# 20 of the edge list's columns taken out of the node table in SBUF by TensorE, and two exponentials inside expert group 3

## The chip, the cores and the metric

The kernel runs on one core of a Trainium2 chip. The metric is the device time of one execution in microseconds; lower is better. The median of 3 runs before the change is 858.64 us.

## The reference, cut to what matters

The model has two layers over 4096 tokens of 64 features (64 images of 64 tokens): wavelet tokens, attention, a mixture of dense experts, a recurrent attention, and at the end a graph step with gated experts. Only the last part is touched.

```python
h = (x_flat @ W_gat).reshape(M, HEADS, NUM_EXPERTS)
e = leaky_relu(a_src[src] + a_dst[dst])            # one row for each edge
ee = exp(e - segment_max(e, dst)[dst])
agg = segment_sum(h[src] * alpha, dst)             # alpha = ee / segment_sum(ee, dst)
scores = layernorm(agg + b_gat).reshape(M, HEADS, NUM_EXPERTS).mean(1)
w = softmax(top_k(scores, 2))
out = sum over 4 experts of w_e * (gelu(x @ W1[e] + b1[e]) @ W2[e] + b2[e])
```

There are 262144 edges drawn over 16384 nodes; the nodes past the 4096 tokens are all alike and are handled apart.

## The kernel before

An earlier stage sorts the edges by destination. Each of the 128 partitions owns 32 nodes (`NC`) and has a list of up to 192 places (`PART`), one edge in each, in the order of the destination. A column of the list is one place on all 128 partitions. In this execution 39 groups of 4 columns (`ASK`) hold edges.

Each node has a row of 24 values (`ROW`): 16 of `h`, 4 source scores and 4 destination scores. The rows are in SBUF, `node_rows_own` in the trace (`G.tab`), node 32p + c at partition p, chunk c; and in HBM, `node_table`. Source rows come from HBM: for each column GpSimd issues one indirect DMA (L2051), which brings 128 rows of 96 bytes into `gathered` (`Gt`). After the last chunk has been written out, 32 more (L2062) bring the rows at the segments' ends.

VectorE does, in this order: a merge over the nodes (`merge`, to L2282), four register reads (`value_load`), then `nodes_of_list` (L2286 to L2312: one-hots of list place against node, counts, and the destination's score for each place, four products over 6144 elements and four sums), then `rows_of_chunk` for three chunks of 64 columns (L2325 to L2350), and for each half of the nodes the merge, the gates and the mixing of the experts' outputs. A chunk waits for its columns (`gat[j]`); then come scores, an exponential on ScalarE (`weights`, L2145), and the running sums (L2342 to L2350), which need the exponential.

Beside that TensorE and ScalarE compute the four experts, without regard to the gates, in four groups of 1024 tokens: `layer1` (L2079), gelu (`hidden`, L2128), `layer2` (L2089), the bias by feature (L2134), the turn back to tokens (L2096) and the copy (`keep_tokens`, L2140). TensorE's order is fixed: layer 1 runs one group and two experts ahead of layer 2. ScalarE's order is fixed as well: the exponential of chunk 0 stands in group 3 behind its first gelus, those of chunks 1 and 2 behind all experts. An engine executes its stream in order; a step that waits holds back all behind it.

## Time and profile before

| | us |
|---|---|
| median of 3 runs (858.08 to 859.08) | 858.64 |
| the profiled execution | 853.77 |
| its span | 851.9 |
| VectorE busy | 601.8 (71%) |
| TensorE matmuls busy | 428.7 (50%) |
| ScalarE busy | 269.5 (32%) |
| GpSimd busy | 189.9 (22%) |

The busy share is a mean over stages that have nothing in common. The last 350 us are the stage of the graph and the experts, and there no engine is busy throughout. Such a stage is read by order of time: for a row, when it starts, how long it takes, and in brackets how long the engine stood idle before it and what ended that. Ends of matmuls are modelled by the profiler, while the start of the step that waits for them is recorded. The name behind an arrow can be "remote" or that of an unrelated transfer where the profile could not match the semaphore.

### The profile page before, as it was taken

To read this page: it belongs to the slowest core of one execution; us is meant where nothing else is said; L and a number is where in the kernel's file an instruction comes from. 1 tells how busy PE (TensorE), PEld (TensorE's weight loads), DVE (VectorE), ACT (ScalarE), POOL (GpSimd) and SP (SyncE) were. 2 spreads that over 40 slices of the span, in tenths; PEclk is the share of its full clock that TensorE was granted. 3 is DMA by queue.
4 is the path that set the end of the run, shared out by engine and by line. 5 is a ranking of instruction groups with operands and counts; after the bars stand their busy time and mean duration, and the time that the engine had idled before them with its cause. 6 is when DMAs were issued, how large, how long until landed. Compare 5 with 4: busy or idle time off the path is not lost.

```text
span 851.9 us, 10421 instructions
## 1 busy us (share of the span) xinstructions
PE 428.7 (50%) x3409; PEld 304.7 (36%) x3409; DVE 601.8 (71%) x2087; ACT 269.5 (32%) x589; POOL 189.9 (22%) x202
## 2 busy tenths in 40 slices
PE   5995575766383669969769827610340110600000
PEld 5874575746372135646657413200110000200000
DVE  3999999977698999877797686999400000670487
ACT  2599678256111222224001324400100001600155
POOL 0100000000000000002000027777777770007600
PEclk9998787896595879988798956955555555655555
DMA  9100000010000000001000000111111130011102
GB/s 200 35 2 1 2 2 2 1 29 2 4 2 0 1 1 2 1 1 32 1 1 1 1 22 9 11 10 10 10 10 10 10 10 1 38 74 9 10 0 49
DMA packets 26681, 13.11 MB, mean 15 GB/s; under 512 B 21161, under 2 KB 25833, under 8 KB 26353
## 3 DMA queue, kind: packets, MB, share of 16 engines
q1 hardware_dynamic: 17696, 9.04, 4.2%
q0 software_dynamic: 6016, 2.32, 3.8%
q10 hardware_dynamic: 2904, 0.98, 0.8%
q8 instruction: 29, 0.48, 0.2%
q14 instruction: 36, 0.29, 0.1%
HBM read 8.43 MB, written 3.90 MB: 14 GB/s over the span
## 4 chain that ended last, share of the span: by engine, by line
another core or an unknown queue 17%; DVE 14%; PE 12%; issue 6%; ACT 3%; POOL 2%; DMA 1%; DVEq 0%; ACTq 0%; POOLq 0%
PE bank L2079 2%; DVE state_x L1780 2%; PE bank L1542 2%; POOL node_rows L2062 2%; PE bank L2089 2%; PE bank L1562 1%; DVE state_x L1777 1%; DVE segment_rows L2347 1%; ACT masked_scores L2128 1%; PE bank L1625 1%; PE bank L1614 1%; PE bank L1602 1%; ACT v_sums_and_norms L2134 1%; DVE v_sums_and_norms L2433 1%
## 5 line engine op out<-in xcount | busy, mean ns | idle before, releaser
L2051 POOL DMA_INDIRECT gathered<-node_table,list_src_i x156 | 151.5, 971 | 153.5 <-issue 153.5
L437 ACT ACTIVATE dst_one_hot<-dst_lo,sign_edges 128x256 bf16<-128x256 bf16 x224 | 90.8, 519 | 16.8 <-PE bank L496 16.8
L2342 DVE TENSOR_TENSOR segment_rows<-gathered,edge_weight_and_decay 128x1024 f32<-128x1024 f32 x3 | 3.7, 1225 | 126.8 <-ACT edge_weight_and_decay L2145 126.8
L496 PE MATMUL bank<-dst_one_hot 128*128 128x128 bf16 x1024 | 72.2, 244 | 38.2 <-DVE dst_one_hot L566 38.2
L496 PEld LDWEIGHTS bank<-dst_one_hot 128*128 128x128 bf16 x1024 | 70.9, 112 | 39.6 <-DVE dst_one_hot L566 39.2
L566 DVE TENSOR_SCALAR dst_one_hot<-dst_hi 128x256 bf16<-128x256 bf16 x512 | 76.3, 388 | 0.3 <-ACT edge_keys_then_tokens L421 0.3
L2096 PE MATMUL bank<-ident,v_sums_and_norms 128*128 128x128 f32 x64 | 13.3, 342 | 98.9 <-ACT v_sums_and_norms L2134 61.9
L2079 PE MATMUL bank<-h_features,e_w 64*128 64x512 f32 x64 | 35.7, 955 | 49.3 <-issue 32.5
L2096 PEld LDWEIGHTS bank<-ident,v_sums_and_norms 128*128 128x128 f32 x64 | 8.5, 169 | 114.4 <-ACT v_sums_and_norms L2134 72.4
L2062 POOL DMA_INDIRECT node_rows<-segment_table,segment_end_i x32 | 30.5, 953 | 73.7 <-DMA segment_table<-segment_rows 64.3
L1080 ACT ACTIVATE z_then_h<-bank,e_B,e_A 128x512 f32<-128x512 f32 x32 | 23.0, 774 | 65.1 <-PE bank L901 65.1
L566 DVE TENSOR_SCALAR dst_one_hot<-dst_lo 128x256 bf16<-128x256 bf16 x288 | 43.0, 390 | 0.0
L2134 ACT ACTIVATE v_sums_and_norms<-bank,e_b_by_feature 128x512 f32<-128x512 f32 x16 | 11.0, 687 | 98.7 <-remote 76.7
L2312 DVE TENSOR_REDUCE edge_dst<-v_sums_and_norms 128x192 f32<-128x6144 f32 x4 | 41.9, 10486 | 0.1
L2079 PEld LDWEIGHTS bank<-h_features,e_w 64*128 64x128 f32 x64 | 13.5, 273 | 67.7 <-issue 40.9
L1206 DVE CUSTOM_DVE_ANT_0 rank_prod_then_keyed<-bank,bin_one_hot 128x128 f32<-128x128 f32 x160 | 34.5, 286 | 0.3 <-DVE slot_key L1198 0.3
L879 POOL PARTITION_ALL_REDUCE bin_max_all<-bin_max x1 | 0.3, 350 | 141.2 <-DVE bin_max L1220 141.2
L926 PE MATMUL bank<-h_and_v_then_places,rank_prod_then_keyed 128*128 128x192 bf16 x320 | 30.4, 257 | 2.2 <-DVE rank_prod_then_keyed L1266 1.9
L926 PEld LDWEIGHTS bank<-h_and_v_then_places,rank_prod_then_keyed 128*128 128x128 bf16 x320 | 28.2, 103 | 8.6 <-DVE rank_prod_then_keyed L1266 6.5
L461 POOL PARTITION_ALL_REDUCE left_max<-left_keys x1 | 0.4, 352 | 137.3 <-DVE left_keys L587 137.3
L2089 PE MATMUL bank<-masked_scores,e_w 128*64 128x512 f32 x64 | 23.6, 855 | 14.1 <-issue 14.1
L2140 ACT COPY state_x<-bank 128x512 f32<-128x512 f32 x16 | 9.3, 584 | 60.2 <-remote 48.7
(452 smaller groups left out, 1071.2 us busy)
## 6 DMA issues: line engine op xcount, KB each, us to landing
gathered<-node_table,list_src_i POOLq DMA_INDIRECT x156
segment_table<-segment_rows SPq DMA_DIRECT2D x3, 768.0 KB, 3.2
dst_one_hot<-in_L_ffn_edge_index SPq DMA_DIRECT2D x2, 1024.0 KB, 7.1
out_dram<-edge_keys_then_tokens SPq DMA_DIRECT2D x4, 256.0 KB, 2.9
images_then_col_weights<-in_x SPq DMA_DIRECT2D x2, 441.0 KB
images_then_col_weights<-in_x ACTq DMA_DIRECT2D x2, 441.0 KB
e_w<-in_L_ffn_W SPq DMA_DIRECT2D x6, 128.0 KB, 4.1
node_rows<-segment_table,segment_end_i POOLq DMA_INDIRECT x32
```

Source lines behind the costliest of these rows:

```text
L437: ins = act.activation(hot[q % 2][:, :, 64 + HOTS + k, :], x, ACT.Sign, bias=edge[:, k:k + 1])
L496: ins = pe.matmul(G.bank[0][:, 0:P], hot[u][:, b, 0:64, i:i + PAIR], hot[u][:, b, 64:P, i:i + PAIR], start=False, stop=True, skip_group_ch ...
L566: ins = dve.tensor_scalar(hot[q % 2][:, :, at + v, :], x, float(v), None, ALU.is_equal)
L926: ins = pe.matmul(sent[:, k * SENT_RANKS:(k + 1) * SENT_RANKS], keyed[:, q % SEND_BUFS, k, i, :], place[:, q % SEND_BUFS, i, :], start=Fal ...
L1080: act.activation(H1[:, n % 2, u, :], G.bank[2 * (n % 2) + u][:, :], ACT.Relu, bias=w.par["B1"][:, q:q + 1], scale=w.par["A1"][:, q:q + 1]) ...
L1206: o.mark(dve.tensor_tensor_reduce(out=prod[:, t, :], in0=count, in1=hot[:, c, :], scale=1.0, scalar=0.0, op0=ALU.mult, op1=ALU.add, accum_ ...
L2051: pool.indirect_dma_start(Gt[:, j, :], None, A["table"], bass.IndirectOffsetOnAxis(ap=G.src_i[:, j:j + 1], axis=0)).then_inc(gat[g // per_ ...
L2062: pool.indirect_dma_start(N[:, c, :], None, A["ends"], bass.IndirectOffsetOnAxis(ap=end_i[:, c:c + 1], axis=0)).then_inc(ends_in[c // H2], 16)
L2079: pe.matmul(G.bank[2 * (n % 2) + u][:, :], W1[r, e, :], G.hT[r, g * TILE:(g + 1) * TILE], start=True, stop=True).then_inc(l1_mm, 1)
L2089: ins = pe.matmul(G.bank[5 + i % 3][rows_of(e), :], W2[:, 2 * pair + e, :], HH[:, u, 2 * pair + e, :], start=True, stop=True, skip_group_c ...
L2096: ins = pe.transpose(G.bank[5 + i % 3][:, h * P:(h + 1) * P], G.by_feature[:, i % 3, h * P:(h + 1) * P], G.ident[:, :])
L2312: f.then(dve.tensor_reduce(AD[:, h, :], by_node.rearrange("p c n -> p n c"), AX_X, ALU.add))
```

## The change

Of the 156 columns that hold edges, 20 (places 4 to 23: `PICK`, groups 1 to 5, `PC` = 4, `PK` = 20) are no longer fetched by GpSimd. They are read from `node_rows_own` in SBUF by matrix products. The number of a source row is split into partition (`low`) and chunk (`high`). TensorE turns `low`, spreads each column over all partitions (20 matmuls), and VectorE compares with the partition's number, which gives a one-hot [node partition x list partition] for each column. For each column two matmuls multiply it with the table's 768 values, into two banks; VectorE multiplies by the one-hot of the chunk and sums over the 32 chunks, which gives the column in `gathered`. All of it stands in VectorE's stream ahead of `nodes_of_list`, and in TensorE's behind the layer-1 matmuls of group 0 and ahead of those of group 1. GpSimd's loop over earlier passes (none in this execution) is split from the last pass, which leaves the 20 columns out, and chunk 0 waits for 20 columns fewer (`asked[NCH]`).

In ScalarE's stream the exponential of chunk 1 moves into expert group 3, behind the gelus of expert 2. The waits for the experts' copies are split by half of the nodes, and `G.gate_tmp` lies in another quarter of the same tile.

```diff
+PICK = range(1, 6)
+PC, PK = PICK.start * ASK, len(PICK) * ASK
...
-    G.gate_tmp = lnv[:, :, :].rearrange("p c d -> p (c d)")[:, 0:3 * NC * 16].rearrange("p (i c f) -> p i c f", i=3, f=16)
+    G.gate_tmp = quarters[:, 0, 0:3 * NC * 16].rearrange("p (i c f) -> p i c f", i=3, f=16)
...
+                if g in by_pe:
+                    continue
...
+        last = passes_but_last(pool)
+        with pool.If(last > 0):
+            with pool.Fori(0, last) as k:
+                list_rows(k, ())
+                node_rows(k)
+        list_rows(last, PICK)
+        node_rows(last)
...
+        def pick_rows():
+
+            pe.wait_ge(gelu_s, 2 * EXP1)
+            pe.wait_ge(low_s, 1)
+            pe.transpose(G.bank[0][0:PK, 0:P], low[:, :], G.ident[:, :]).then_inc(low_mm, 1)
+            pe.wait_ge(lowT_s, 1)
+            for b in range(len(PICK)):
+                for i in range(4):
+                    ins = pe.matmul(G.bank[SPREAD[b]][:, i * P:(i + 1) * P],
+                                    G.ident[0:PK, 4 * b + i:4 * b + i + 1].to_broadcast([PK, P]), low_T, start=True,
+                                    stop=True, skip_group_check=True)
+                ins.then_inc(spread_mm, 1)
+            for j in range(PK):
+                pe.wait_ge(hot_s, 1 if j == 0 else len(PICK))
+                if j >= 3:
+                    pe.wait_ge(pick_s, j - 2)
+                for i, b in enumerate(pick_banks(j)):
+                    ins = pe.matmul(G.bank[b][:, 0:NC // 2 * ROW], hot_rows[:, j, :],
+                                    flat_tab[:, i * (NC // 2 * ROW):(i + 1) * (NC // 2 * ROW)], start=True, stop=True)
+                ins.then_inc(pick_mm, 1)
+            pe.wait_ge(pick_s, PK)
...
         for n in range(NG * EXP1):
+            if n == EXP1:
+                pick_rows()
             layer1(n)
...
-            act.wait_ge(x_s, 4 * NG)
+            act.wait_ge(x_s, 2 * NG * (g + 1))
...
                 hidden(g, e)
+                if g == NG - 1 and e == 2:
+                    weights(last, 1)
...
-        for j in range(1, NCH):
-            weights(last, j)
+        weights(last, NCH - 1)
...
+    def pick_rows_of_list(dve, f):
+
+        c = slice(PC, PC + PK)
+        f.mark(dve.tensor_scalar(low_i[:, :], G.src_i[:, c], 5, None, ALU.arith_shift_right))
+        f.then(dve.tensor_scalar(high_i[:, :], G.src_i[:, c], NC - 1, NC, ALU.bitwise_and, ALU.bitwise_or))
+        f.then(dve.tensor_copy(low[:, :], low_i[:, :]))
+        f.mark(dve.tensor_copy(high[:, :], high_i[:, :]))
+        f.then(dve.tensor_scalar(low[:, :], low[:, :], float(PART), None, ALU.mult))
+        dve.sem_inc(low_s, 1)
...
+        for j in range(PK):
+            dve.wait_ge(pick_mm, j + 1)
+            for i, b in enumerate(G.pick_banks(j)):
+                h = slice(i * (NC // 2), (i + 1) * (NC // 2))
+                f.mark(dve.tensor_tensor(picked[:, j % 2, :, h],
+                                         G.bank[b][:, 0:NC // 2 * ROW].rearrange("p (c f) -> p f c", f=ROW),
+                                         hot_high[:, j, h].unsqueeze(1).to_broadcast([P, ROW, NC // 2]), ALU.mult))
+            f.wait()
+            dve.sem_inc(pick_s, 1)
+            f.mark(dve.tensor_reduce(Gt[:, PC + j, :], picked[:, j % 2, :, :], AX_X, ALU.add))
+        f.wait()
...
+        pick_rows_of_list(dve, f)
         nodes_of_list(dve, f)
-        rows_of_chunk(dve, f, last, 0, asked[0])
+        rows_of_chunk(dve, f, last, 0, asked[NCH])
...
-        dve.wait_ge(x_s, 4 * NG)
         merge_half(dve, f, last, 0)
```

TensorE, from the turn of the tokens to the first layer-2 steps of the experts; the number behind x counts matmuls in a row. Before:

```order
L2109 MATMUL bank<-ident,e_b 128x1 x2
L2079 MATMUL bank<-h_features,e_w 128x512 x12
L2089 MATMUL bank<-masked_scores,e_w 64x512 x4
L2096 MATMUL bank<-ident,v_sums_and_norms 128x128 x4
L2089 MATMUL bank<-masked_scores,e_w 64x512 x2
L2096 MATMUL bank<-ident,v_sums_and_norms 128x128 x4
L2089 MATMUL bank<-masked_scores,e_w 64x512 x2
L2096 MATMUL bank<-ident,v_sums_and_norms 128x128 x8
```

After:

```order
L2164 MATMUL bank<-ident,e_b 128x1 x2
L2108 MATMUL bank<-h_features,e_w 128x512 x8
L2143 MATMUL bank<-ident,picked_row_low 20x128
L2147 MATMUL bank<-v_sums_and_norms,ident 128x128 x20
L2156 MATMUL bank<-node_rows_own,v_sums_and_norms 128x384 x40
L2108 MATMUL bank<-h_features,e_w 128x512 x4
L2118 MATMUL bank<-masked_scores,e_w 64x512 x4
L2125 MATMUL bank<-ident,v_sums_and_norms 128x128 x4
L2118 MATMUL bank<-masked_scores,e_w 64x512 x2
L2125 MATMUL bank<-ident,v_sums_and_norms 128x128 x4
```

One transpose, 20 spreading matmuls and 40 picking ones stand between the eighth and the ninth layer-1 matmul.

VectorE, from the branch behind the merge (the untaken loop over earlier passes) into `nodes_of_list`. Before:

```order
L2450 COMPARE_AND_BRANCH
L2449 UNCONDITIONAL_BRANCH
L2286 CAST list_node<-list_place_i 128x192
L147 ISA
L2287 CAST list_node_bf16<-list_node 128x192
L2288 TENSOR_TENSOR same_as_before<-list_node 128x191
```

After, the last two of the 20 columns and what follows (`v_sums_and_norms` is the tile in which one-hots and products lie):

```order
L2365 TENSOR_TENSOR v_sums_and_norms<-bank0,v_sums_and_norms 128x24x16
L2365 TENSOR_TENSOR v_sums_and_norms<-bank7,v_sums_and_norms 128x24x16
L149 REGISTER_ALU
L2370 TENSOR_REDUCE gathered<-v_sums_and_norms 128x24
L2365 TENSOR_TENSOR v_sums_and_norms<-bank1,v_sums_and_norms 128x24x16
L2365 TENSOR_TENSOR v_sums_and_norms<-bank2,v_sums_and_norms 128x24x16
L149 REGISTER_ALU
L2370 TENSOR_REDUCE gathered<-v_sums_and_norms 128x24
L149 REGISTER_ALU
L2375 CAST list_node<-list_place_i 128x192
L149 REGISTER_ALU
L2376 CAST list_node_bf16<-list_node 128x192
```

The pair of products and the sum come 20 times, each pair behind a wait for TensorE; only then follows what stood at this place before.

ScalarE in expert group 3, from the exponential of chunk 0. Before:

```order
L2144 ISA
L2145 ACT_TABLE_LOAD
L2145 ACTIVATE edge_weight_and_decay<-edge_weight_and_decay 128x512
L2128 ACT_TABLE_LOAD
L2128 ACTIVATE masked_scores<-bank,e_b 128x512 x6
L2134 ACTIVATE v_sums_and_norms<-bank,e_b_by_feature 128x512 x2
L2140 COPY state_x<-bank 128x4x128
L2134 ACTIVATE v_sums_and_norms<-bank,e_b_by_feature 128x512
L2140 COPY state_x<-bank 128x4x128
L2134 ACTIVATE v_sums_and_norms<-bank,e_b_by_feature 128x512
L2140 COPY state_x<-bank 128x4x128 x2
L2144 REGISTER_ALU
```

After:

```order
L2201 ISA
L2202 ACT_TABLE_LOAD
L2202 ACTIVATE edge_weight_and_decay<-edge_weight_and_decay 128x512
L2185 ACT_TABLE_LOAD
L2185 ACTIVATE masked_scores<-bank,e_b 128x512 x4
L2201 REGISTER_ALU
L2202 ACT_TABLE_LOAD
L2202 ACTIVATE edge_weight_and_decay<-edge_weight_and_decay 128x512
L2185 ACT_TABLE_LOAD
L2185 ACTIVATE masked_scores<-bank,e_b 128x512 x2
L2191 ACTIVATE v_sums_and_norms<-bank,e_b_by_feature 128x512 x2
L2197 COPY state_x<-bank 128x4x128
```

The exponential of chunk 1 now stands between the gelus of expert 2 and expert 3, with a table load of its own on either side.

## Rows read from the trace of the kernel before

**Rows 1.** Page, costliest groups: line engine op out<-in xcount | busy us, mean ns | idle before
```profile
L2051 POOL DMA_INDIRECT gathered<-node_table,list_src_i x156 | 151.5, 971 | 153.5 <-issue 153.5
...
L2089 PE MATMUL bank<-masked_scores,e_w 128*64 128x512 f32 x64 | 23.6, 855 | 14.1 <-issue 14.1
```

**Rows 2.** Order of time, GpSimd: start us, us, engine, line, op [idle before <-releaser]
```profile
505.25 0.95 POOL L2051 DMA_INDIRECT gathered<-node_table,list_src_i  x1 [0.30 <-issue]
...
524.42 3.17 POOL L2051 DMA_INDIRECT gathered<-node_table,list_src_i  x1 [0.31 <-issue]
...
701.43 0.94 POOL L2051 DMA_INDIRECT gathered<-node_table,list_src_i  x1 [0.30 <-issue]
```

**Rows 3.** Order of time, VectorE, 494 to 606 us
```profile
494.64 0.55 DVE L1825 TENSOR_TENSOR node_rows_own<-bank,lnw_n_inv 128x384 f32<-128x384 f32 x1
...
497.79 0.96 DVE L1831 TENSOR_TENSOR node_rows_own<-node_rows_own,table_of_tokens 128x768 f32<-128x768 f32 x1 [0.22 <-DVE lnh_n_sum L239]
...
522.34 0.26 DVE L2286 CAST list_node<-list_place_i 128x192 f32<-128x192 int32 x1 [5.60 <-issue]
...
523.42 3.35 DVE L2290 TENSOR_TENSOR list_node_one_hot<-list_node_bf,nodes_twice 128x6144 bf16<-128x6144 bf16 x1
...
601.31 1.00 DVE L2325 TENSOR_TENSOR_SCAN edge_max_so_far<-before_penalty,gathered 128x64 f32<-128x64 f32 x4 [0.19 <-issue]
```

**Rows 4.** Order of time, VectorE, 727 to 763 us
```profile
727.38 1.23 DVE L2342 TENSOR_TENSOR segment_rows<-gathered,edge_weight_and_decay 128x1024 f32<-128x1024 f32 x1 [121.47 <-ACT edge_weight_and_decay L2145]
...
733.37 1.24 DVE L2325 TENSOR_TENSOR_SCAN edge_max_so_far<-before_penalty,edge_max_so_far,gathered 128x64 f32<-128x64 f32 x4 [0.24 <-DVE segment_rows L2350]
...
742.84 1.22 DVE L2342 TENSOR_TENSOR segment_rows<-gathered,edge_weight_and_decay 128x1024 f32<-128x1024 f32 x1 [4.63 <-ACT edge_weight_and_decay L2145]
...
750.03 1.23 DVE L2325 TENSOR_TENSOR_SCAN edge_max_so_far<-before_penalty,edge_max_so_far,gathered 128x64 f32<-128x64 f32 x4 [0.23 <-DVE segment_rows L2350]
...
755.62 1.23 DVE L2342 TENSOR_TENSOR segment_rows<-gathered,edge_weight_and_decay 128x1024 f32<-128x1024 f32 x1 [0.75 <-ACT edge_weight_and_decay L2145]
...
761.48 1.10 DVE L2350 TENSOR_TENSOR_SCAN segment_rows<-edge_weight_and_decay,segment_rows 128x64 f32<-128x64 f32 x4
```

**Rows 5.** Order of time, ScalarE, 596 to 741 us
```profile
596.96 1.27 ACT L2128 ACTIVATE masked_scores<-bank,e_b 128x512 f32<-128x512 f32 x2
...
614.68 0.69 ACT L2128 ACTIVATE masked_scores<-bank,e_b 128x512 f32<-128x512 f32 x1 [3.85 <-DMA bin_slots<-empty_slots]
...
630.78 0.69 ACT L2128 ACTIVATE masked_scores<-bank,e_b 128x512 f32<-128x512 f32 x1 [4.91 <-DMA bin_slots<-empty_slots]
664.38 0.69 ACT L2134 ACTIVATE v_sums_and_norms<-bank,e_b_by_feature 128x512 f32<-128x512 f32 x1 [32.91 <-remote]
674.88 0.69 ACT L2134 ACTIVATE v_sums_and_norms<-bank,e_b_by_feature 128x512 f32<-128x512 f32 x1 [9.82 <-remote]
...
718.28 0.69 ACT L2134 ACTIVATE v_sums_and_norms<-bank,e_b_by_feature 128x512 f32<-128x512 f32 x1 [9.90 <-remote]
...
723.66 1.27 ACT L2128 ACTIVATE masked_scores<-bank,e_b 128x512 f32<-128x512 f32 x2
...
728.66 2.42 ACT L2128 ACTIVATE masked_scores<-bank,e_b 128x512 f32<-128x512 f32 x4
...
740.28 0.58 ACT L2140 COPY state_x<-bank 128x512 f32<-128x512 f32 x1 [0.27 <-PE bank L2096]
```

**Rows 6.** Order of time, TensorE matmuls, 541 to 637 us
```profile
541.68 1.94 PE L2089 MATMUL bank<-masked_scores,e_w 128*64 128x512 f32 x8
544.72 0.66 PE L2096 MATMUL bank<-ident,v_sums_and_norms 128*128 128x128 f32 x4 [1.10 <-issue]
...
633.52 3.37 PE L2089 MATMUL bank<-masked_scores,e_w 128*64 128x512 f32 x8
```

**Rows 7.** Windows: us, busy us (x) of PE, PEld, DVE, ACT, POOL, granted clock, DMA
```profile
505.00:544.00 39.00, 27.42 (x84) 11.74 (x84) 31.73 (x58) 16.76 (x29) 30.22 (x29) 0.72 0.10 10
544.00:718.00 174.00, 30.63 (x68) 10.24 (x68) 61.38 (x19) 13.38 (x21) 119.98 (x127) 0.53 0.14 9
```

More of the change, by code:

```diff
@@ L806, in attention0_sort_and_experts0 @@
         r_g = st.sb("groups_f", [P, 1])
-        asked = st.sb("asked_f", [P, NCH])
+        asked = st.sb("asked_f", [P, NCH + 1])
         over = st.sb("more_than_sent", [P, 2])
@@ L1237, in sizes @@
                     f.wait()
+                    f.mark(dve.tensor_scalar(asked[:, NCH:NCH + 1], r_g[:, :], -1.0, float(len(PICK)), ALU.add, ALU.min))
+                    f.wait()
+                    f.then(dve.tensor_tensor(asked[:, NCH:NCH + 1], asked[:, 0:1], asked[:, NCH:NCH + 1], ALU.subtract))
                     f.then(dve.tensor_scalar(asked[:, :], asked[:, :], 16.0 * ASK, 16.0, ALU.mult, ALU.max))
@@ L1937, in graph_and_experts @@
     Gt = G.gathered
+    low_i, high_i = sb("picked_row_low_i", [P, PK], I32), sb("picked_row_high_i", [P, PK], I32)
+    low, high = sb("picked_row_low", [P, PK]), sb("picked_row_high", [P, PK])
+    hot_rows = G.by_node[:, 0:PK * P].rearrange("p (j m) -> p j m", m=P)
+    picked = G.by_node[:, PK * P:PK * P + 2 * NC * ROW].rearrange("p (i f c) -> p i f c", i=2, f=ROW)
+    hot_high = G.by_node[:, 4096:4096 + PK * NC].rearrange("p (j c) -> p j c", c=NC)
+    low_T = G.by_node[0:PK, 4096 + PK * NC:4096 + PK * NC + P]
+    flat_tab = G.tab[:, :, :].rearrange("p c f -> p (c f)")
+    low_s, low_mm, lowT_s, spread_mm, hot_s, pick_mm, pick_s = (
+        sem("picked_low_ready"), sem("picked_low_turned"), sem("picked_low_by_column"), sem("picked_low_spread"),
+        sem("picked_one_hot"), sem("picked_rows_mm"), sem("picked_rows_taken"))
     AD = sb("edge_dst", [P, HEADS, PART])
@@ L1993, in graph_and_experts @@
     BY_ACT = range(2, EXP1)
+    SPREAD = (1, 2, 3, 5, 6)
     def part_of(e, c):
@@ L2037, in _ @@
         pool.iota(row_i[:, :], [[0, NC]], base=0, channel_multiplier=PART).then_inc(iota_s, 1)
-        n = passes(pool)
         m = pool.value_load(G.groups[0:1, 0:1], min_val=1, max_val=fold)
@@ L2041, in _, with list_rows @@
         pool.sem_inc(seen, 1)
-        with pool.Fori(0, n) as k:
+        def list_rows(k, by_pe):
             pool.wait_ge(list_ready, k + 1)
@@ L2058, in _, with node_rows @@
                                                 ).then_inc(gat[g // per_chunk], 16)
+        def node_rows(k):
             pool.wait_ge(rows_out, 16 * NCH * k + 16 * NCH)
@@ L2105, in layer2_of_group, with pick_banks @@
             to_tokens(4 * g + 3)
+        def pick_banks(j):
+            return ((0, 7), (1, 2), (3, 5))[j % 3]
+        def pick_rows():
[18 more added lines that the diff above has]
+            pe.wait_ge(pick_s, PK)
+        G.pick_banks = pick_banks
         pe.wait_ge(w2_s, 4)
@@ L2282, in merge @@
         f.then(dve.tensor_tensor(agg[:, c, :], agg[:, c, :], t16[:, c, :], ALU.add))
+    def pick_rows_of_list(dve, f):
[6 more added lines that the diff above has]
+        dve.sem_inc(low_s, 1)
+        f.mark(dve.tensor_tensor(hot_high, high[:, :].unsqueeze(2).to_broadcast([P, PK, NC]),
+                                 nodes[:, :, 0].unsqueeze(1).to_broadcast([P, PK, NC]), ALU.is_equal))
+        dve.wait_ge(low_mm, 1)
+        f.then(dve.tensor_copy(low_T, G.bank[0][0:PK, 0:P]))
+        dve.sem_inc(lowT_s, 1)
+        for b in range(len(PICK)):
+            dve.wait_ge(spread_mm, b + 1)
+            f.then(dve.tensor_scalar(hot_rows[:, 4 * b:4 * b + 4, :].rearrange("p j m -> p (j m)"),
+                                     G.bank[SPREAD[b]][:, :], rowf[:, 0:1], None, ALU.is_equal))
+            dve.sem_inc(hot_s, 1)
+        for j in range(PK):
[8 more added lines that the diff above has]
+            f.mark(dve.tensor_reduce(Gt[:, PC + j, :], picked[:, j % 2, :, :], AX_X, ALU.add))
+        f.wait()
     def nodes_of_list(dve, f):
@@ L2418, in _ @@
         last = passes_but_last(dve)
-        asked = [dve.value_load(G.asked[0:1, j:j + 1], min_val=16, max_val=16 * CW) for j in range(NCH)]
+        asked = [dve.value_load(G.asked[0:1, j:j + 1], min_val=16, max_val=16 * CW) for j in range(NCH + 1)]
         def first_experts(g):
             c = half(g)
+            dve.wait_ge(x_s, 2 * NG * (g + 1))
             for e in range(BY_ACT.start):
@@ L2508, in program @@
         G.passes = st.sb("graph_passes", [P, 1], I32)
-        G.asked = st.sb("rows_asked", [P, NCH], I32)
+        G.asked = st.sb("rows_asked", [P, NCH + 1], I32)
         G.earlier = st.sb("graph_passes_but_last", [P, 1], I32)
```

## The prediction

> **What bounds the kernel now.** I read the costliest groups first, then the order of time of each engine from 500 us on, then two windows. GpSimd fetches 156 of the list's columns from the node table in HBM, one indirect DMA each [rows 1]; they run back to back at 1.25 us from about 504 us and end at 702.4 us [rows 2]. VectorE is not the limit there: it has the first chunk's exponents ready at 605.9 us and then sits idle for 121.47 us until ScalarE has taken the exponential [rows 3, 4]. So the question is what keeps ScalarE. Its expert steps are not long (0.69 us) but stand 10 us apart [rows 5], and what they wait for are matmuls. TensorE's own rows show those matmuls early: eight entries of the second expert layer start at 633.52 us and would be over at 636.9, yet the two ScalarE steps that read them start at 664.38 and 674.88 us [rows 5, 6]. The completion of a matmul reaches its waiter late, and at a steady pace: from 664.38 to 718.28 us there are five steps of 10.8 us, and between two of them four TensorE entries stand in program order. That is **2.7 us for one entry**, however short it is. (An fp32 matmul is two entries: the code has 32 of the second layer, the page 64.) The windows say the same: 84 entries in the 39 us to 544, then 68 in 174 us, 2.6 us each [rows 7]. This holding begins at about 544 us, 40 us after the first gather, and ends between 718.28 and 723.66 us, 16 to 21 us after the last [rows 2, 5]. From there on all runs at normal pace: the exponential, the first chunk's rows at 727.38, and the chain to 762.6 us [rows 4], behind which the node rows and the gates follow. The kernel is thus bounded by matmul completions that are held while GpSimd gathers, and by the end of the gathers that releases them.
>
> **The gathers, 20 fewer.** Nothing else on GpSimd's stream goes: 20 x 1.25 = 25 us. The wait of GpSimd's next step, the node rows, still ends with VectorE's third chunk. The new code tests once for earlier passes and jumps over their loop; I take 1 us. The last gather ends at 702.4 - 25 + 1 = 678. One gather took 3.17 us, beside VectorE's large one-hot comparison [rows 2, 3], which now comes later than the gathers: I take 2 us off, 676. The release is then at 692 to 697, I take 694.
>
> The Trainium skill, SBUF — State Buffer (Who interferes with whom), says that a VectorE instruction with two SBUF inputs contends with a GpSimd instruction that reads SBUF. By that rule the comparison does delay the gather, and the trace agrees at this one place; without it the release would come 2 us later and nothing else would change.
>
> **Before the picks.** VectorE reads four registers in 5.60 us of idle time ahead of 522.34 [rows 3]; a fifth read adds 1.4, so it is free at 523.7. Six small instructions and one comparison over 640 elements (nearest row: 0.96 for 768) take 2.5 us. TensorE stands behind the last gelu of expert group 0 (about 526 us) and then does one transpose and 20 spreading matmuls, 40 entries at 0.16 to 0.24 us (the 128-column entries at 544.72, four in 0.66, and the 512-column ones at 541.68, eight in 1.94 [rows 6]), 8 us, 9 with the handovers. The first pick can start at about 536 us.
>
> **One picked column** is two matmuls, 4 entries, for TensorE; for VectorE two products of 384 elements out of PSUM (0.55 each) and one sum over 768 elements (0.96) [rows 3], with gaps 2.2 us. If nothing were held, 20 columns would take 44 us, end at 580, and hide behind the 121 us in which VectorE idles. But each column waits for the completion of its 4 entries, and by [rows 5] that is 4 x 2.7 = **10.8 us** once the holding has begun. Three pairs of banks let TensorE run ahead, which does not help against a pace. The trace has no VectorE waiting for TensorE in this stretch, so the price is bounded: 2.2 us from below, 10.8 from above, and up to 14 if the three waits that TensorE issues per column count as entries too. I take 10.8, since the delay goes with TensorE's entries and not with ScalarE's steps: two gelus whose matmuls were issued long before run back to back at 596.96 in the middle of the holding, and where only two entries stand between gelus (614.68 to 630.78, three steps) the pace is 5.4 [rows 5].
>
> Until 544 us: (544 - 536) / 2.2 = 4 columns. From 544 to 694: 150 / 10.8 = 14. The last 2 after the release: 4 us. **The picks end at 698 us.**
>
> **What is queued behind them.** On VectorE the list's one-hots and the destination scores: from 522.34 to 601.31 us, 79.0 us [rows 3], of plain VectorE work that has hidden behind the idle time. It cannot start before 698, so ends at 777. The cover is gone, and that is the loss. On TensorE expert layer 1 from the fifth matmul on, and all of layer 2. After the release ScalarE passes 14 expert steps in about 12.2 us (728.66 to 740.86, [rows 5]); three groups of 16 need at most 60 us, to 758, behind the 79 us of VectorE. Costed at nothing for that reason.
>
> **The chunks.** Chunk 0: scores 4.6 us (601.31 to 605.91), exponential with its handover 0.76, rows 6.0 (727.38 to 733.37). Chunk 1: scores 4.85, exponential 0.76, rows 7.2 (742.84 to 750.03). Chunk 2: 4.85, 0.76, 7.0. Sum 36.8 [rows 3, 4]; 777 + 36.8 = 813.8.
>
> **The second exponential inside group 3.** In the kernel before it waits for ScalarE's last expert copy at 740.28, which costs VectorE 4.63 us [rows 4, 5]. In the sum above this idle time is already left out. The move costs ScalarE one more pair of table loads; the third exponential then has to follow the last copies. VectorE asks for the second at 777 + 4.6 + 0.76 + 6.0 + 4.85 = 793.2 and for the third 0.76 + 7.2 + 4.85 later, at 806.0. ScalarE in between: two table loads and two gelus some 4, eight layer-2 steps 7 to 8 at the pace of [rows 5]: 805.5. Just in time; I add 0.7.
>
> **Sum.** The chain reaches 814.5 instead of 762.6: +51.9 us. The tail from 762.6 is unchanged; the scratch that moves to another quarter and the experts' waits that are split in halves change no duration, since both have long been met. The profiled execution took 853.77 (span 851.9); it would take 905.7. The runs shown have a median 4.87 us above it, so 858.64 + 51.9 = **910 us**, and this is the likeliest.
>
> **Rivals.** (A) The forecast. Its own range: if 8 columns are through before the holding, the last 12 need 130 us, the picks end at 674 and the time is 886; if a column costs 14 us and 6 are left at the release, the picks end at 707, and with a release some us later 930.
> (B) The picks are not held: the delay belongs to what ScalarE waits for, not to TensorE. For it: in the trace only ScalarE is seen waiting. Against: the pace follows the number of TensorE entries (10.8 for 4, 5.4 for 2). Then picks end at 580, the scores at 659, but the experts of group 0 start 50 us later: 42 steps before the first exponential, 14 of them at 8 us until 694, 28 at 0.87: 719 instead of about 726.7, and 4.6 off for the second exponential: 12 us faster, **847**.
> (C) The gathers' end alone sets the time and everything behind it moves with it: 25 us less, **833**. Against it: the matmuls that were held are still to be made, and there are 121 entries more. The NOTIFIC block's page of the Trainium skill (NOTIFIC — the notification-queue block, Overflow) says that the block's internal pipeline holds back the engine rather than lose a record. If that were the cause, runs without records would not be held and would follow C; but the median of the runs shown is above the profiled execution, not some 45 us below it (702.4 to 750.03, where chunk 2 could have begun, is 48 us), so the numbers speak against; I give that reading 0.02 of C's chance.
> (D) Picks partly held, ending near 645: the sum breaks even there (645 + 79 + 36.8 + 1 is 762). Between 640 and 650 the change is within 0.2%. It needs 11 columns before the holding, where I count 4.
> The tipping point of the whole is this: picks that end later than 645 us lose, whatever the gathers save.
>
> **Numbers.** A 0.70; picks ending between 650 and 670, 0.05 (slower too, 862 to 882); D 0.05; B 0.13; C or faster 0.07. Faster 0.20, same 0.05, slower 0.75; 0.2% is about what a measurement of this kernel tells from no change. The range must reach over D to B to leave out no more than 2 in 10: 843 to 930; A alone is 880 to 930.
>
> **What would show it.** Right: the gather rows are 136 and end near 677; VectorE's products out of PSUM stand some 11 us apart from about 545 on, waiting for TensorE, and 2.2 us apart before and after; the one-hot comparison starts near 700 and chunk 0's scores near 777; no idle time of 100 us is left on VectorE. Wrong: picks at 2.2 us throughout, ending by 585 (B or C); or a holding that starts later than 560 us.

## The result, and the profile after

| us | before | after |
|---|---|---|
| median | 858.46 (4 runs, 858.08 to 859.08) | 933.78 (4 runs, 922.79 to 939.36) |
| profiled execution | 853.77 | 934.16 |
| its span | 851.9 | 932.3 |

The ratio is 1.087 (1.079 to 1.095): the changed kernel is 75 us slower by the medians. (The two profiled executions lie 80.4 us apart; that of before is 4.7 us below its median.) 910 was forecast, and 933.78 lies 4 us above the range. Direction and mechanism came as described, the size did not.

GpSimd's side answers to [rows 1, 2]: 136 gathers, the last at 676.22 us (page, then order of time).

```profile
L2070 POOL DMA_INDIRECT gathered<-node_table,list_src_i x136 | 129.1, 949 | 149.9 <-issue 149.9
...
506.92 1.29 POOL L2070 DMA_INDIRECT gathered<-node_table,list_src_i  x1 [108.72 <-issue]
...
676.22 0.94 POOL L2070 DMA_INDIRECT gathered<-node_table,list_src_i  x1 [0.30 <-issue]
```

VectorE of the changed kernel in order of time, which answers to [rows 3, 4]. L2358 makes the one-hots of four columns out of a bank that four spreading matmuls filled; L2365 is the product of a picked column; L2375 begins the list's one-hots and scores; L2414 and L2431 are a chunk's scores and the rows behind its exponential.

```profile
538.18 0.75 DVE L2358 TENSOR_SCALAR v_sums_and_norms<-bank,list_row 128x512 f32<-128x512 f32 x1 [13.98 <-remote]
559.88 0.75 DVE L2358 TENSOR_SCALAR v_sums_and_norms<-bank,list_row 128x512 f32<-128x512 f32 x1 [20.95 <-issue]
...
627.08 0.75 DVE L2358 TENSOR_SCALAR v_sums_and_norms<-bank,list_row 128x512 f32<-128x512 f32 x1 [21.65 <-issue]
638.98 1.02 DVE L2365 TENSOR_TENSOR v_sums_and_norms<-bank,v_sums_and_norms 128x384 f32<-128x384 f32 x2 [11.15 <-remote]
...
650.17 1.02 DVE L2365 TENSOR_TENSOR v_sums_and_norms<-bank,v_sums_and_norms 128x384 f32<-128x384 f32 x2 [9.08 <-remote]
...
692.90 1.02 DVE L2365 TENSOR_TENSOR v_sums_and_norms<-bank,v_sums_and_norms 128x384 f32<-128x384 f32 x2 [8.38 <-remote]
...
697.83 1.02 DVE L2365 TENSOR_TENSOR v_sums_and_norms<-bank,v_sums_and_norms 128x384 f32<-128x384 f32 x2 [2.81 <-PE bank L2156]
...
724.18 1.01 DVE L2365 TENSOR_TENSOR v_sums_and_norms<-bank,v_sums_and_norms 128x384 f32<-128x384 f32 x2
...
726.33 0.26 DVE L2375 CAST list_node<-list_place_i 128x192 f32<-128x192 int32 x1
...
805.32 0.99 DVE L2414 TENSOR_TENSOR_SCAN edge_max_so_far<-before_penalty,gathered 128x64 f32<-128x64 f32 x4 [0.19 <-DVE edge_dst L2401]
...
841.28 1.10 DVE L2439 TENSOR_TENSOR_SCAN segment_rows<-edge_weight_and_decay,segment_rows 128x64 f32<-128x64 f32 x4
```

The reader is to see three stretches. From 538 to 627 us the five banks stand some 22 us apart, the last four 22.4: (627.08 - 559.88) / 3. From 639 to 693 us six columns stand 10.8 us apart: (692.90 - 638.98) / 5. From 697.83 on thirteen more follow, 2.03 us apart. The idle time of 121.47 us [rows 4] is gone, and the list's scores, which used to hide behind it, end at 805.32.

TensorE's starts, which answer to [rows 6], show that the matmuls themselves were not slow:

```profile
524.31 8.04 PE L2147 MATMUL bank<-v_sums_and_norms,ident 20*128 20x128 f32 x36 [0.80 <-issue]
533.97 0.36 PE L2147 MATMUL bank<-v_sums_and_norms,ident 20*128 20x128 f32 x1 [1.61 <-issue]
...
547.26 0.80 PE L2156 MATMUL bank<-node_rows_own,v_sums_and_norms 128*128 128x384 f32 x1 [2.00 <-issue]
550.06 0.80 PE L2156 MATMUL bank<-node_rows_own,v_sums_and_norms 128*128 128x384 f32 x1 [2.00 <-issue]
627.94 5.49 PE L2156 MATMUL bank<-node_rows_own,v_sums_and_norms 128*128 128x384 f32 x8 [77.08 <-issue]
```

36 of the 40 spreading entries run in 8.04 us, as the prediction had it. But VectorE, which waits for the first eight of them, is served at 538.18 and for the next eight at 559.88.

ScalarE, against [rows 5]: idle for 207.55 us, then the experts at normal pace, then a wait for VectorE.

```profile
730.06 1.48 ACT L2191 ACTIVATE v_sums_and_norms<-bank,e_b_by_feature 128x512 f32<-128x512 f32 x2 [207.55 <-PE bank L2118]
...
810.01 0.63 ACT L2202 ACTIVATE edge_weight_and_decay<-edge_weight_and_decay 128x512 f32<-128x512 f32 x1 [46.67 <-DVEq L2429]
```

### The profile page after: what moved, and what is told of

It is laid out like the page before. It is cut to its first block, busy times and chain, and to the rows that moved or that the text cites. A ratio compares the mean times of both kernels' runs of the same rounds, so it can differ in the third digit from the quotient of the medians.

```text
span 932.3 us, 10791 instructions
## 1 busy us (share of the span) xinstructions
PE 469.2 (50%) x3530; PEld 327.7 (35%) x3530; DVE 645.4 (69%) x2161; ACT 270.8 (29%) x591; POOL 167.6 (18%) x182
## 4 chain that ended last, share of the span: by engine, by line
DVE 26%; issue 13%; another core or an unknown queue 8%; PE 7%; POOL 2%; ACT 1%; DMA 1%; DVEq 1%; POOLq 0%
DVE edge_dst L2401 5%; DVE v_sums_and_norms L2399 3%; DVE state_x L1785 2%; DVE v_sums_and_norms L2365 2%; PE bank L1547 2%; POOL node_rows L2083 2%; DVE state_x L1782 1%; PE bank L1567 1%; DVE segment_rows L2436 1%; DVE gathered L2370 1%; PE bank L1630 1%; PE bank L1607 1%; PE bank L1619 1%; DVE v_sums_and_norms L2523 1%
## 5 line engine op out<-in xcount | busy, mean ns | idle before, releaser
L2070 POOL DMA_INDIRECT gathered<-node_table,list_src_i x136 | 129.1, 949 | 149.9 <-issue 149.9
L2156 PE MATMUL bank<-node_rows_own,v_sums_and_norms 128*128 128x384 f32 x80 | 44.9, 707 | 136.0 <-issue 116.5
L2156 PEld LDWEIGHTS bank<-node_rows_own,v_sums_and_norms 128*128 128x128 f32 x80 | 20.0, 268 | 161.8 <-issue 159.3
L2358 DVE TENSOR_SCALAR v_sums_and_norms<-bank,list_row 128x512 f32<-128x512 f32 x5 | 3.7, 749 | 99.9 <-issue 85.9
L2365 DVE TENSOR_TENSOR v_sums_and_norms<-bank,v_sums_and_norms 128x384 f32<-128x384 f32 x40 | 20.3, 548 | 57.3 <-remote 54.5
L2108 PE MATMUL bank<-h_features,e_w 64*128 64x512 f32 x64 | 25.5, 769 | 65.0 <-ACT masked_scores L2185 51.9
L2108 PEld LDWEIGHTS bank<-h_features,e_w 64*128 64x128 f32 x64 | 9.7, 219 | 76.6 <-ACT masked_scores L2185 60.2
L1597 PE MATMUL bank<-state_x 128*128 128x128 f32 x128 | 21.6, 339 | 11.8 <-DVEq L1787 11.8
L2399 DVE TENSOR_TENSOR v_sums_and_norms<-list_node_one_hot,bank 128x6144 f32<-128x6144 bf16 x4 | 26.2, 6554 | 0.1
```

Source lines behind the costliest of these rows:

```text
L2070: pool.indirect_dma_start(Gt[:, j, :], None, A["table"], bass.IndirectOffsetOnAxis(ap=G.src_i[:, j:j + 1], axis=0)).then_inc(gat[g // per_ ...
L2108: pe.matmul(G.bank[2 * (n % 2) + u][:, :], W1[r, e, :], G.hT[r, g * TILE:(g + 1) * TILE], start=True, stop=True).then_inc(l1_mm, 1)
L2156: ins = pe.matmul(G.bank[b][:, 0:NC // 2 * ROW], hot_rows[:, j, :], flat_tab[:, i * (NC // 2 * ROW):(i + 1) * (NC // 2 * ROW)], start=True ...
L2365: f.mark(dve.tensor_tensor(picked[:, j % 2, :, h], G.bank[b][:, 0:NC // 2 * ROW].rearrange("p (c f) -> p f c", f=ROW), hot_high[:, j, h].u ...
L2399: f.then(dve.tensor_tensor(by_node, at_node[:, :, :], own_score[:, :, h:h + 1].to_broadcast([P, NC, PART]), ALU.mult))
```

## The experiments

**Two kinds of sets.** The kernels ran in seven sets, each on one chip and each with the kernel before in it. The same kernel before took 858.5, 859.6, 858.5 and 858.4 us in four sets and 804.7, 804.8 and 805.4 us in three others. In the first kind completions are held as described. In the second nothing is held. It is no property of the chip: chip 9 gave a held set and, seven minutes later, a free one. A row of the page tells them apart, the issues of the gathers: x, and the median time from issue to landing, here for the kernel before (first kind) and for the early exponentials (E6, second kind).

```profile
gathered<-node_table,list_src_i POOLq DMA_INDIRECT x156
```
```profile
gathered<-node_table,list_src_i POOLq DMA_INDIRECT x156, 2.4
```

In the held sets the page has no landing time for the gathers, since most of their landing records are missing. So it is in all 10 traces of held sets, while all 10 of free sets have the 2.4. I call them held and free sets, and compare kernels of two sets only by their ratios to the kernel before, or by their traces.

### E5: the gathers behind the picks (held set)

```diff
+        pool.wait_ge(pick_s, PK)
         list_rows(last, PICK)
```

> The changed kernel, but GpSimd waits with its first gather until VectorE has taken the last picked column. Theory (H), the gathers hold the completions: nothing is held between 524 and the first gather, the spreading takes 9 us, the columns are 2.0 us apart from the first to the last, and the picks end near 575 us instead of 726. The 136 gathers then run from 576 to about 746. The holding can only start some 25 us or more after 576; TensorE needs about 40 us for the other three expert groups, so at most a part of them is held. If the exponential of chunk 0 still comes by 746, the chain ends about 13 us behind the last gather, near 760, and the time is about that of the kernel before, 850 to 865; if the rest of the experts is held, up to 900. Rival (U), the matmuls of the picks are slow by themselves or through VectorE's or ScalarE's work: the picks end at 726 again, the gathers behind them at 896, and the time is near 1000.

Measured: 902.19 us in one run. GpSimd, VectorE's first and last column, and ScalarE:

```profile
583.72 1.29 POOL L2070 DMA_INDIRECT gathered<-node_table,list_src_i  x1 [183.94 <-issue]
```
```profile
543.06 1.02 DVE L2366 TENSOR_TENSOR v_sums_and_norms<-bank,v_sums_and_norms 128x384 f32<-128x384 f32 x2 [2.11 <-PE bank L2157]
...
581.60 1.01 DVE L2366 TENSOR_TENSOR v_sums_and_norms<-bank,v_sums_and_norms 128x384 f32<-128x384 f32 x2
```
```profile
601.62 0.69 ACT L2192 ACTIVATE v_sums_and_norms<-bank,e_b_by_feature 128x512 f32<-128x512 f32 x1 [0.17 <-issue]
605.62 0.59 ACT L2198 COPY state_x<-bank 128x512 f32<-128x512 f32 x1 [3.32 <-remote]
...
633.80 0.59 ACT L2198 COPY state_x<-bank 128x512 f32<-128x512 f32 x1 [10.54 <-remote]
```

(This stage begins some 8 us later here than in the profile of after, as in some other executions below.) With no gather under way a column takes 2.03 us, (581.60 - 543.06) / 19, and all that VectorE does for the picks 54 us where it took 204. The holding has moved with the gathers: it begins 19 to 22 us after the first one (the step at 605.62 is the first late one, and waits from 602.3 on). So the gathers are needed for it, and the picks' matmuls aren't slow by themselves. The rest of the experts was held instead, the exponential of chunk 0 came at 777.24, and the time is 2 us above the upper case expected.

### E7 and E3: what one unit of holding is (held set)

E7 makes two matmuls of 192 columns out of each of 384; E3 makes one spreading matmul of 512 columns out of four of 128.

```diff
-                    ins = pe.matmul(G.bank[b][:, 0:NC // 2 * ROW], hot_rows[:, j, :],
-                                    flat_tab[:, i * (NC // 2 * ROW):(i + 1) * (NC // 2 * ROW)], start=True, stop=True)
+                    for q in range(2):
+                        w = NC // 4 * ROW
+                        ins = pe.matmul(G.bank[b][:, q * w:(q + 1) * w], hot_rows[:, j, :],
+                                        flat_tab[:, (2 * i + q) * w:(2 * i + q + 1) * w], ...
```

> The changed kernel, but each of the 40 picking matmuls is two of 192 columns: the same data, banks and signals, 8 TensorE entries for a column in place of 4. Theory (H), per entry: the held columns stand 21.6 to 22.4 us apart instead of 10.8, about 3 of them are through by the release near 697, 17 follow at 2.0 to 2.6 us, the picks end at 732 to 742, and the time is 5 to 15 us above the changed kernel. Rival (Z), per data or per signal: 10.8 us apart as before, time unchanged.

```diff
-                for i in range(4):
-                    ins = pe.matmul(G.bank[SPREAD[b]][:, i * P:(i + 1) * P],
-                                    G.ident[0:PK, 4 * b + i:4 * b + i + 1].to_broadcast([PK, P]), low_T, ...
+                pe.matmul(G.bank[SPREAD[b]][:, :], ones_k, G.by_node[0:PK, 4 * b * P:4 * (b + 1) * P], ...
```

> The changed kernel, but the 20 spreading matmuls of 128 columns are 5 of 512 columns (rows masked by the identity against an all-ones matrix): the same numbers, the same five banks and five semaphore increments, a quarter of the TensorE entries (10 for 40), and one VectorE product over 2560 elements more (about 3 us). Theory (H), one held completion per entry at 2.8 us: the banks come about 5.6 us apart instead of 22.4, the spreading ends near 560 us instead of 627, the picks follow 10.8 us apart and have about 6 more columns through by the release near 697; they end at about 714 instead of 726, and the time is 12 us below the changed kernel, about 922. Rival (Z), the delay goes with the data written to a bank or with each signal: the banks stay about 22 us apart and the time is that of the changed kernel, or 3 us more.

Measured: E7 942.04 us (one run); E3 912.92 us (4 runs, 911.8 to 915.14; 1.0625 of before, 1.056 to 1.069). VectorE of E7, then of E3:

```profile
650.76 1.02 DVE L2368 TENSOR_TENSOR v_sums_and_norms<-bank,v_sums_and_norms 128x384 f32<-128x384 f32 x2 [21.65 <-remote]
...
673.86 1.02 DVE L2368 TENSOR_TENSOR v_sums_and_norms<-bank,v_sums_and_norms 128x384 f32<-128x384 f32 x2 [20.98 <-issue]
```
```profile
536.93 0.75 DVE L2359 TENSOR_SCALAR v_sums_and_norms<-bank,list_row 128x512 f32<-128x512 f32 x1 [0.96 <-PE bank L2147]
...
544.33 1.01 DVE L2366 TENSOR_TENSOR v_sums_and_norms<-bank,v_sums_and_norms 128x384 f32<-128x384 f32 x2
...
550.49 1.02 DVE L2366 TENSOR_TENSOR v_sums_and_norms<-bank,v_sums_and_norms 128x384 f32<-128x384 f32 x2 [4.05 <-remote]
...
561.01 1.02 DVE L2366 TENSOR_TENSOR v_sums_and_norms<-bank,v_sums_and_norms 128x384 f32<-128x384 f32 x2 [8.41 <-remote]
```

The same data in twice the entries: 23.1 us a column in place of 10.8, and the picks end at 733. The trace shows this; the time of the one run lies only 3 us above the highest of the changed kernel. The same data in a quarter of the entries: the spreading is over at 537.7 and not at 627.8. Data and signals are as in the changed kernel in both, so the unit is the **TensorE entry, 2.7 to 2.9 us each**, and rival Z falls. (Each matmul entry has a weight load of its own; the runs don't tell the two apart.) E3 also corrects theory H: I expected its banks 5.6 us apart, and they came 1.7 us apart, with three columns more before the holding at about 546. With five spreading matmuls instead of twenty the picks end at 705 and not at 726: 21 us, as the ratios have it (1.0625 and 1.087). Even so E3 loses 53 us to the kernel before.

### E18, E4, E11: half of the gathers

```diff
+                if g >= 20:
+                    continue
...
-        dve.wait_ge(gat[j], k * (16 * CW) + count)
+        if j < 2:
+            dve.wait_ge(gat[j], k * (16 * CW) + count)
```

> The kernel before with 80 gathers instead of 156 (places 80 to 155 of the list are left out of the result), a last time, for a held set. If this set is held: theory (H), the 10.8 us pace ends at 620 to 626 and the time is 770 to 785 beside 859; rival (U) 859. If it is not held: 721 to 728 beside 804.

Measured in the held set: 769.1 us. In two free sets the same kernel (E4, E11) took 727.46 and 721.31. GpSimd and ScalarE of E18:

```profile
611.27 0.94 POOL L2053 DMA_INDIRECT gathered<-node_table,list_src_i  x1 [0.30 <-issue]
```
```profile
602.29 0.69 ACT L2136 ACTIVATE v_sums_and_norms<-bank,e_b_by_feature 128x512 f32<-128x512 f32 x1 [9.81 <-remote]
614.91 0.59 ACT L2142 COPY state_x<-bank 128x512 f32<-128x512 f32 x1 [11.94 <-remote]
621.22 0.69 ACT L2136 ACTIVATE v_sums_and_norms<-bank,e_b_by_feature 128x512 f32<-128x512 f32 x1 [5.72 <-remote]
621.95 0.59 ACT L2142 COPY state_x<-bank 128x512 f32<-128x512 f32 x1
```

The holding ends with the gathers, 100 us earlier than in the kernel before, and the exponential of chunk 0 came at 639.91. Rival U would have kept the slow pace to 718. The release, between 614.91 and 621.22, lies 3 to 9 us behind the end of the last gather (612.2) here, not 16 to 21: that distance is no constant.

### E9 and E14: the changed kernel again

> The changed kernel itself, beside the kernel before. In one set of runs the kernel before took 859.6 us and TensorE's completions were held during the gathers; in another it took 804.7 us, nothing was held, and the trace has 4303 records of landed transfers where the held one has 1929. If this set is a held one: 923 to 939 against 859, as first measured. If it is not held, theory (H) says the loss was all holding: spreading 9 us, columns 2.0 us apart, picks end near 577 us, the list's scores near 656, chunk 0 near 668, and from there the chain hangs on the gathers, which end 24 us earlier than those of the kernel before: 775 to 785 against 804, faster. Rival (V), the picks cost VectorE's and TensorE's time in any case: 804 or more. No held completion and a kernel that is still slower would refute H.

Measured: a held set, 935.34 us (4 runs, 933.45 to 936.8) beside 858.49; 1.089 (1.086 to 1.092). The first result stands.

> The changed kernel, for a set in which nothing is held; two sets so far were held (933.8 and 935.3 beside 858.5). If this set is held: 923 to 940 again. If it is not held: theory (H) 775 to 785 beside 804, since the chain then hangs on the last gather, 24 us earlier; rival (V) 804 or more.

Measured: a free set, **782.66 us (4 runs, 780.18 to 784.24) beside 804.76; 0.974 (0.970 to 0.979)**. There the change is 22 us faster. VectorE:

```profile
528.40 0.75 DVE L2358 TENSOR_SCALAR v_sums_and_norms<-bank,list_row 128x512 f32<-128x512 f32 x1 [0.96 <-PE bank L2147]
531.26 1.02 DVE L2365 TENSOR_TENSOR v_sums_and_norms<-bank,v_sums_and_norms 128x384 f32<-128x384 f32 x2 [2.11 <-PE bank L2156]
...
570.20 1.01 DVE L2365 TENSOR_TENSOR v_sums_and_norms<-bank,v_sums_and_norms 128x384 f32<-128x384 f32 x2
...
686.12 1.24 DVE L2414 TENSOR_TENSOR_SCAN edge_max_so_far<-before_penalty,edge_max_so_far,gathered 128x64 f32<-128x64 f32 x4 [10.82 <-DMA gathered<-node_table,list_src_i]
```

The picks end at 572, the scores of the list at 651, and the last chunk waits 10.82 us for gathered columns: now the gathers bound the chain, and 20 fewer are worth 22 us, close to the 25 of the prediction's rival C. Rival V falls. Without the holding there is no loss.

### E6 and E10: the exponentials ahead in ScalarE's stream

The kernel before, with the three exponentials moved. This tests the reading of [rows 4, 5] on the unchanged work.

```diff
-            if g == NG - 1:
+            if g == 2:
                 weights(last, 0)
...
                 if i > 4 * g:
                     keep_tokens(i - 1)
+                if i == 9:
+                    weights(last, 1)
+                if i == 10:
+                    weights(last, 2)
         keep_tokens(4 * NG - 1)
-        for j in range(1, NCH):
-            weights(last, j)
```

> The kernel before, with ScalarE's three exponentials moved forward in its stream only: that of chunk 0 behind the token copy in group 2 (609 us in the trace of before), that of chunk 1 behind the copy that stands at 686, that of chunk 2 behind the one at 708. The work on every engine is the same. Theory (H): VectorE's 121 us of idle time are the wait behind held expert steps, nothing else. With the exponentials ahead of the expert steps, the chunks end about 10 to 13 us after the last gather, at 712 to 718 instead of 762.6, and the time is 810 to 820. Sub-case: the node rows are then gathered from about 720 on, beside the last expert steps; if these are held again, 820 to 850. Rival (C): the chain behind the gathers is bound by something other than ScalarE's order: 858.

Measured: a free set, 804.51 us (10 runs, 802.91 to 809.99) beside 804.74; no difference (0.993 to 1.001). Neither the theory's number nor a verdict for rival C: with nothing held no exponential is late.

> The kernel before with the three exponentials ahead in ScalarE's stream, once more, since the set it first ran in had nothing held. If this set is held: theory (H) 810 to 820 against 859 (up to 850 if the last expert steps are held beside the node rows' gathers), rival (C) 859. If it is not held: 804 as the kernel before, again.

Measured: a held set, **820.69 us (5 runs, 818.48 to 840.47) beside 858.49; 0.955 (0.952 to 0.958)**. The time is at the upper edge of what was expected. VectorE, from the profiled execution, which is one of the two longer ones (span 832.7, gathers from 510.36 to 711.22):

```profile
638.15 1.26 DVE L2344 TENSOR_TENSOR segment_rows<-gathered,edge_weight_and_decay 128x1024 f32<-128x1024 f32 x1 [25.62 <-issue]
...
717.27 1.22 DVE L2344 TENSOR_TENSOR segment_rows<-gathered,edge_weight_and_decay 128x1024 f32<-128x1024 f32 x1 [34.18 <-ACT edge_weight_and_decay L2145]
...
739.66 1.10 DVE L2352 TENSOR_TENSOR_SCAN segment_rows<-edge_weight_and_decay,segment_rows 128x64 f32<-128x64 f32 x4
```

No engine has less to do, only the order changes, and 38 us go. The chunks end 29 us after the last gather instead of 60. This version beats the kernel before where completions are held, and costs nothing where they aren't.

### E2, E1, E12, E16: the second exponential by itself

E2 is the changed kernel without the move, E1 (and again E12 and E16) the kernel before with it.

```diff
+                if g == NG - 1 and e == 2:
+                    weights(last, 1)
```

> The changed kernel, but the exponential of chunk 1 stands where it stood before, behind all expert steps. Theory (H): nearly all of the 75 us come from the picks, whose matmuls are held while GpSimd gathers; the exponential is worth only what chunk 1 would wait for the last expert copies. In the changed kernel ScalarE is free for chunk 1 at 822.24 us; with the expert steps of group 3 ahead of it (14 steps in about 12.2 us from 811) it comes at 824 to 828. So 2 to 6 us slower than the changed kernel, 935 to 940, and the picks unchanged. Rival (X): the exponential inside group 3 and its table loads are what costs; then this kernel is near 860.

Measured: a held set, 938.05 us (4 runs, 936.76 to 939.26), 1.092 of before (1.086 to 1.099), against 933.8 and 935.3 for the changed kernel in other held sets. VectorE waits 4.41 us for chunk 1's exponential there, and 0.75 in the changed kernel. So by the waits the move is worth 3.7 us; the times don't tell it from nothing, since the intervals of the ratios overlap. The picks cost all of the rest.

> The kernel before, with only the exponential of chunk 1 moved into expert group 3, behind the gelus of expert 2. Theory (H): it takes away the 4.63 us in which VectorE waits for it, and costs a pair of table loads that ScalarE has time for: 854, 4 us faster. Rival (X): the third exponential, which has to follow the last expert copies, comes late by as much: 858 or a few us more.

Measured: free sets only, 803.41 (12 runs), 804.5 (10 runs) and 804.96 us (10 runs) beside 804.74, 804.76 and 805.41; 0.996 (0.993 to 0.999), 1.000 (0.998 to 1.002) and 1.000 (0.996 to 1.004): next to nothing, as expected where no exponential is late. What the move is worth alone in a held set stays untested.

### E17, E8, E13, E15: four columns and early exponentials

The early exponentials with 4 columns picked, spread by one matmul (`PICK = range(1, 2)`).

> The kernel of the early exponentials with 4 columns picked by TensorE instead of 20, spread by one matmul. Theory (H): 1 + 2 + 16 TensorE entries and their signals; with each held at 2.8 us the picks end at 560 to 580 us, the list's scores end 79 us later at 640 to 660, chunk 0 still ends before chunk 1's columns are there, and the gathers end 4 us earlier (4 x 1.25 - 1): 3 to 5 us faster than the kernel with the early exponentials alone. Rival (L): the expert steps behind the picks come so much later that they take the place of the gathers as the bound behind the release: 5 to 25 us slower than it.

> Early exponentials and 4 columns picked by TensorE, a last time, for a held set: three sets so far had nothing held (803.4 to 803.7). If this set is held: theory (H) 812 to 822; rival (L), the expert steps late by the picks and chunk 1's exponential behind them, 825 to 850. If it is not held: 803 to 804.

Measured: 803.72, 803.36 and 803.66 us in free sets, as the kernel before (each interval takes in 1). In a held set 862.42 us (10 runs, 856.96 to 867.0) beside 858.39; 1.004 (1.000 to 1.008). The gain of the early exponentials is lost. ScalarE:

```profile
615.73 0.69 ACT L2189 ACTIVATE v_sums_and_norms<-bank,e_b_by_feature 128x512 f32<-128x512 f32 x1 [82.87 <-issue]
...
738.46 0.63 ACT L2200 ACTIVATE edge_weight_and_decay<-edge_weight_and_decay 128x512 f32<-128x512 f32 x1
```

The picks end at 583.4 and the list's scores at 662, 2 to 3 us later than the latest expected. But the first expert steps of group 0 come at 615.73 where they came at 536.62 in E10, and with them the exponential of chunk 0: at 738.46, not 637.49. This is rival L, and stronger than I priced it. From the last gelu of group 0, at 532, up to that step TensorE has 31 entries (19 of the picks, 8 of layer 1, 4 of layer 2), and 31 x 2.7 is 84 us: 616. While completions are held, every entry put ahead of the experts delays all of them by its 2.7 us.

## Why the prediction was right and where it failed

| step | predicted | measured |
|---|---|---|
| last gather issued | 676 end | 677.2 end |
| VectorE free for the picks | 523.7 | 522.3 |
| **spreading matmuls served** | **by 536 (9 us)** | **627.1 (103 us)** |
| a held column | 10.8 | 10.8 |
| release | 694 (692 to 697) | between 692.9 and 697.8 |
| columns through by then | 18 | 6 |
| a column not held | 2.2 | 2.03 |
| picks end | 698 | 726.3 |
| list's scores | 79.0 | 79.0 |
| chunks, with the exponentials | 37.5 | 37.1 |
| experts behind the scores | hidden | hidden, ScalarE waits 46.67 |
| chain against before | +51.9 | +79.8 |

The durations but one are right to 2 us; the columns through, the end of the picks and the chain are off by what follows from that one. The step that failed is the sentence on the 20 spreading matmuls, "40 entries at 0.16 to 0.24 us [...], 8 us, 9 with the handovers". It priced them by TensorE's own rows, while the paragraph behind it priced the picks by their completions. The rule that the prediction had read from [rows 5, 6], 2.7 us for one entry however short, holds for them as well: five banks of 8 entries at 2.8 us. With 108 us in place of 9 the same sum lets the picks start at 536 + 99 = 635, has 5.5 columns through at 694 and the other 14.5 by 726: 28 us more. That is 938 from the median, and 933.7 from the profiled execution, where 934.16 was measured. The measured +79.8 less +51.9 is 27.9, all of it in this step (726.3 - 698 = 28.3).

Why it was missed: the onset of the holding was taken as a time, 544 us, 40 us after the first gather, from one case, and the spreading was to be over by then. The runs show it 19 to 22 us behind the first gather in E5, 17 to 31 in the changed kernel (first gather at 506.92; the copy of the transpose comes at once, at 523.93, the first bank late, at 538.18), and 37 to 43 in E3. What decides it is open; E3, with few entries in a burst, has it late. The range of forecast A reached only to a later release and to a dearer column. It never let the spreading be held, though no row of before bounded its completion from above.

Rival B (the delay belongs to ScalarE's waits) is refuted by VectorE's waits of 20 us and by E7. Rival D's tipping point, picks ending at 645, was passed by 81 us. Rival C was priced nearly right, at 25 us, for the other condition: the free set gives 22. The 2 us for the gather beside the one-hot comparison were right too: in E14, where the comparison runs beside the gathers, one of them takes 3.17 us at 574.46; in the held profile of after, where it follows them, none takes over 1.4.

One argument of the prediction proves nothing. It held the reading that only recording delays the completions to be unlikely, since the median of the runs isn't below the profiled execution. But each of these runs left a span and a granted clock, so none is without records. Whether an execution without any is held stays open, and with it how much of the 75 us would be left in one.

The traces make this reading more likely than the 0.02 it was given. The landing records are missing in exactly the sets that are held. Up to 480 us the trace of before (held) and that of E12 (free) have as many records of semaphore updates, 2496 and 2498; from 560 to 700 us, while the gathers run, they have 201 and 1847, which is 1.4 per us against 13. All held traces have 1.4 per us beside their gathers, whatever the kernel: one record in 0.7 us. Four times that is the 2.8 us of a TensorE entry, and twice that is the 1.4 us between VectorE's late steps shown below. So the engines may be waiting for a recording path of that pace. This is argued, not shown.

## What to carry to other kernels

Where a profile shows completions that reach their waiters at a fixed pace, price every instruction of that engine by the pace, the short preparatory ones first: their count matters, not their size. Look for what is queued behind the slow waiter and doesn't need it; moving three exponentials in an in-order stream gave 38 us where taking away 20 transfers cost 75. And run the kernel before anew in each set: the same change was 8.7% slower and 2.6% faster on one and the same kernel, by a condition that the page shows in one missing number. All these times are of recorded executions.

## What the runs showed of the hardware

- While GpSimd issues indirect DMAs (1.25 us apart), the completions of TensorE's entries reached VectorE or ScalarE 2.7 to 2.9 us apart in four sets, and at once in three sets.
- TensorE runs on ahead: in the changed kernel 36 entries started within 8.04 us, then starts 1.4 to 2.8 us apart.
- VectorE's dependent steps are late too while the node rows are gathered in a held set. In E10:

```profile
774.53 0.43 DVE L2379 TENSOR_TENSOR node_agg<-node_agg,gat_bias 128x256 f32<-128x256 f32 x1 [0.97 <-DVE node_agg L2376]
775.92 0.42 DVE L2380 TENSOR_REDUCE gate_s<-node_agg 128x16 f32<-128x256 f32 x1 [0.97 <-DVE node_agg L2379]
```

  Steps of 0.43 us stand 1.4 us apart. In the free E12 the same steps stand 0.46 us apart:

```profile
753.92 0.42 DVE L2378 TENSOR_TENSOR node_agg<-node_agg,gat_bias 128x256 f32<-128x256 f32 x1
754.38 0.42 DVE L2379 TENSOR_REDUCE gate_s<-node_agg 128x16 f32<-128x256 f32 x1
```

  Behind the chunks the span has 89.9 us in the changed kernel in the held set, and 79.6 in the free one (778.3 - 698.7).
- The Trainium skill, NOTIFIC — the notification-queue block (Overflow: three behaviours, one of which stalls the engine), says that the block's internal pipeline always backpressures rather than losing a record inside the block. The late completions agree with that. The held sets lack records at the same time (1929 of landed transfers in the trace of before, 4303 in that of E6, with as many gathers), which that sentence alone doesn't give. The cause of the two conditions is not settled.
